# Decoder layer on one core: attention in two halves of 256 tokens with a state between them, and silu as one ScalarE function

## The reference

```python
qkv = silu(x @ qkv_w.T)                      # 32 heads of q, k, v, 128 wide
# linear attention with a decay per head, here written over all pairs of tokens
scores[n, m] = (q[n] . k[m]) * exp(-slope * (n - m))   if n >= m else 0
attn = scores @ v                            # the reference steps over blocks of 64 with a state
attn = attn * rsqrt(mean(attn ** 2) + 1e-5)  # over all heads
x = layernorm(x + (sigmoid(x @ gate_w.T) * norm_w * attn) @ out_w.T)
x = layernorm(x + fake_quant(x) @ fake_quant(ctx_4096))
x = layernorm(x + grouped_ffn(x))            # 16 groups, gelu
```

## Time and profile before

| | us |
|---|---|
| median of three runs (1871.03 to 1873.51) | 1873.34 |
| span of the profiled execution | 1870.5 |
| TensorE busy | 1807.6 (97%) |
| VectorE busy | 1443.7 (77%) |
| ScalarE busy | 940.1 (50%) |
| GpSimd busy | 627.6 (34%) |

### The profile page before, as it was taken

One profiled execution on the slowest core, in us unless ns is written; L12 is line 12 of the kernel. 1 busy time (PEld: TensorE's weight loads), 2 busy tenths in 40 slices (PEclk: granted clock), 3 DMA queues, 4 the chain that ended last, 5 costly groups with the idle time before them and its releaser, 6 DMA issues.

```text
span 1870.5 us, 26340 instructions
## 1 busy us (share of the span) xinstructions
PE 1807.6 (97%) x9325; PEld 872.7 (47%) x9325; DVE 1443.7 (77%) x2029; ACT 940.1 (50%) x1402; POOL 627.6 (34%) x506
## 2 busy tenths in 40 slices
PE   6999999999999999999999999999999999998887
PEld 4444544444444544444444544444444544564433
DVE  7777777778777777778777777778777777669877
ACT  5554544545454545545454545445354544434664
POOL 2352334324342334324342334324342332301423
PEclk9999999999999999999999999999999999999998
DMA  4112223131322223221321213121221213133332
GB/s 174 65 68 91 69 90 90 69 90 46 119 63 90 69 89 91 76 83 46 119 62 57 70 56 90 57 68 46 85 63 57 71 54 91 58 103 122 113 91 90
DMA packets 117792, 149.64 MB, mean 80 GB/s; under 512 B 67232, under 2 KB 83744, under 8 KB 117280
## 3 DMA queue, kind: packets, MB, share of 16 engines
q1 hardware_dynamic: 106208, 135.29, 22.9%
q0 software_dynamic: 2560, 8.39, 1.4%
q10 hardware_dynamic: 8896, 4.28, 0.8%
HBM read 119.63 MB, written 12.58 MB: 71 GB/s over the span
## 4 chain that ended last, share of the span: by engine, by line
PE 77%; DVE 13%; ACT 4%; issue 4%; DMA 1%; POOL 0%; ACTq 0%; DVEq 0%; SPq 0%; POOLq 0%
PE bank L1296 18%; PE bank L1298 17%; PE bank L1297 17%; PE bank L1269 6%; PE bank L1361 4%; PE bank L1363 3%; PE bank L1362 3%; DVE gated_split L1616 3%; PE bank L1338 2%; PE bank L1340 2%; PE bank L1339 2%; DVE acc L1758 2%; PE bank L1425 1%; PE bank L1436 1%; DVE bank L1676 1%
## 5 line engine op out<-in xcount | busy, mean ns | idle before, releaser
L1296 PE MATMUL bank<-x_blocks,w_pair 128*128 128x512 f16 (+1 forms) x1820 | 678.5, 373 | 12.7 <-DVE bank L1664 7.3
L1298 PE MATMUL bank<-x_blocks,w_pair 128*128 128x512 f16 (+1 forms) x1820 | 678.3, 373 | 0.0
L1297 PE MATMUL bank<-x_blocks,w_pair 128*128 128x512 f16 (+1 forms) x1820 | 678.2, 373 | 0.0
L1876 POOL TENSOR_TENSOR sums_pair<-raw_pair 128x512 f32<-128x512 f32 x63 | 87.0, 1380 | 576.5 <-DVE w_pair L1616 414.6
L1296 PEld LDWEIGHTS bank<-x_blocks,w_pair 128*128 128x128 f16 x1820 | 177.9, 98 | 218.2 <-DVE bank L1664 15.0
L1298 PEld LDWEIGHTS bank<-x_blocks,w_pair 128*128 128x128 f16 x1820 | 178.0, 98 | 202.8
L1297 PEld LDWEIGHTS bank<-x_blocks,w_pair 128*128 128x128 f16 x1820 | 178.1, 98 | 191.0
L1758 DVE TENSOR_TENSOR acc<-acc,bank 128x512 f32<-128x512 f32 x320 | 207.8, 680 | 17.5 <-PE bank L1363 17.5
L1537 ACT ACTIVATE scores_split<-bank 128x512 f16<-128x512 f32 (+1 forms) x192 | 100.6, 526 | 180.9 <-DVE bank L1721 160.7
L1616 DVE SCALAR_TENSOR_TENSOR w_pair<-raw_pair,w_pair 128x1024 f16<-128x1024 f32 x126 | 158.0, 1273 | 34.3 <-ACT w_pair L1489 34.1
L1902 POOL TENSOR_TENSOR ssq<-ssq,sig 128x512 f32<-128x512 f32 x64 | 83.4, 1303 | 282.4 <-ACT sig L1543 281.9
(11 more groups left out here) (212 smaller groups left out, 2637.4 us busy)
## 6 DMA issues: line engine op xcount, KB each, us to landing
raw_pair<-w_qk SPq DMA_DIRECT2D x32, 1024.0 KB, 5.0
raw_pair<-w_gate SPq DMA_DIRECT2D x16, 1024.0 KB, 4.9
raw_pair<-w_out SPq DMA_DIRECT2D x16, 1024.0 KB, 4.9
raw_pair<-w_vt SPq DMA_DIRECT2D x15, 1024.0 KB, 4.9
decay_sb<-decay SPq DMA_DIRECT2D x32, 256.0 KB, 5.3
raw_pair<-ctx_in SPq DMA_DIRECT2D x8, 1024.0 KB, 4.8
acc<-x_t SPq DMA_DIRECT2D x4, 1024.0 KB, 11.5
ctx<-raw_pair SPq DMA_DIRECT2D x8, 512.0 KB, 3.4
```

What stands on the lines that cost most here:

```text
L1296: pe.matmul(out, w_hi, x_hi, start=unmet and k == 0, stop=False, skip_group_check=halves or not fresh)
L1297: pe.matmul(out, w_hi, x_lo, start=False, stop=False, skip_group_check=halves or not fresh)
L1298: mm = pe.matmul(out, w_lo, x_hi, start=False, stop=k == QT - 1, skip_group_check=halves or not fresh)
```

## The change

Silu: ScalarE computes the function Silu straight into `sig32` and the two halves are split from there; the VectorE multiply goes, and a bank is free after ScalarE's one read. `sig32` is held until the low half is written.

Attention of pairs 0 to 14: the 512 tokens are taken in two halves of 256. Scores are computed within each half only (256 and 128 columns for each of two key blocks, in two groups). What the second half takes from the first goes through a state of 128 x 128 per unit. The keys of the first half are multiplied by their decay to the half's end on GpSimd (`k_decay`), split (ScalarE, VectorE) and turned by a DMA transpose on SP (`k_turn`); `state` multiplies them with the values on TensorE and its result is split (ScalarE, VectorE); `attend` multiplies the state with the queries of the second half into a second bank, VectorE scales it by the queries' decay (`inter`) and adds it to bank 7 (`joined`), and only then ScalarE squares. The decay rates (128 KB each, two for the keys and two for the queries of a pair) are loaded by SP, and the decay tiles shrink from 256 to 128 KB. Pair 15 keeps the whole attention.

Order: `state(0)` stands behind the first `gate` product, `state(1)` behind `score(2)`; `gated(0)` and `gated(2)` stand behind the next unit's scores; `gate_rest` (two sigmoids) comes before `units(3)` in `q` instead of after stage 1; the products of `v` run 1, 7, 2, 6, 4, 5, 3. `g32` of all four units lies in the key tile. Core of the diff:

```diff
+HALF_GROUPS = ((0, 2), (1, 3))
+H_OFF = {0: 0, 2: HT, 1: 2 * HT, 3: 2 * HT + P}
+N_HALF = 2 * (HT + P)
...
-    "k": {"p1": "e10", "p6": "w1 w2 l", "p3": "c w0"},
+    "k": {"p1": "e10", "p6": "w1 w2 l", "p5": "j0", "p3": "c w0 j1"},
...
-        st = self.add("silu", done=done, place=place, sign=sign, gi=gi, sig_free=self.sig_free[gi], sig=self.tick("sig"),
-                      silu=self.tick("silu"), dst=dst, free=dst_free if isinstance(dst_free, list) else [dst_free],
-                      slot=self.late_slot, hi=self.tick("qkv_hi"))
-        self.sig_free[gi] = st["silu"]
-        return self.tick("qkv_lo")
+        st = self.add("silu", done=done, place=place, sign=sign, gi=gi, sig_free=self.sig_free[gi], silu=self.tick("silu"),
+                      dst=dst, free=dst_free if isinstance(dst_free, list) else [dst_free], slot=self.late_slot,
+                      hi=self.tick("qkv_hi"))
+        lo = self.sig_free[gi] = self.tick("qkv_lo")
+        return gi, st["silu"], lo
...
+        gi, silu, lo = self.silu(done, place, sign, (which, r), [self.qk_free, self.g_split] if which == "k" else
+                                 [self.qk_free, self.q_read])
+        self.release(place, silu)
+        if which == "k" and r % 2 == 0:
+            self.decay_keys(r // 2, gi, lo)
         for b in range(B):
...
+    def decay_keys(self, g, gi, lo):
+
+        self.add("k_decay", g=g, gi=gi, lo=lo, rate=self.rate_ready[g])
+        rate = self.rate_free[g] = self.sig_free[gi] = self.tick("k_rate")
+        self.kd[g] = gi, rate
+
+    def turn_keys(self, g):
+
+        gi, rate = self.kd[g]
+        self.add("k_turn", g=g, gi=gi, rate=rate, free=self.s_free, hi=self.tick("kd_hi"), before=self.q_read)
+        lo = self.sig_free[gi] = self.tick("kd_lo")
+        self.steps[-1]["lo"] = lo
+        self.s_free = self.k_turned[g] = self.tick(f"k_turned{g}", 16)
+
+    def state(self, g):
+
+        i, bank, free = self.main_ring.take()
+        self.add("state", g=g, bank=bank, free=free, turned=self.k_turned[g], v=[t for b in range(B) for t in self.v_done[b][g]],
+                 mm=self.tick("state_mm"), hi=self.tick("st_hi"))
+        self.st_done[g] = self.tick("st_lo")
+        self.main_ring.give(i, self.st_done[g])
+
     def kv_out(self, b, r):
 
         done, place, sign = self.result(r)
-        lo = self.silu(done, place, sign, ("kv", b, r), [self.qk_free, self.g_split, self.late_units_free])
-        self.release(place, lo)
+        _, silu, lo = self.silu(done, place, sign, ("kv", b, r), [self.qk_free, self.g_split, self.late_units_free])
...
+        if not whole:
+            j, st["bank2"], st["free2"] = self.main_ring.take()
+            st["state"], st["rate"] = self.st_done[h % GH], self.rate_ready[h % GH]
+            st["inter_mm"], st["inter"], st["joined"] = self.tick("inter_mm"), self.tick("inter"), self.tick("joined")
+            self.main_ring.give(j, st["inter"])
+            self.rate_free[h % GH] = st["inter"]
+            self.q_read = st["mm"]
         self.s_free = st["mm"]
...
-        if unit == 0:
-            free = [self.g_split, self.g_summed]
-        else:
-            free = [self.scores_mm[1 if unit < 3 else 3]]
...
-                 blocked=blocked, free=free if blocked else [])
+                 blocked=blocked, free=[self.scores_mm[1 if unit < 2 else 3]] if blocked else [])
...
+    def load_rates(self, n, what):
+
+        for g in range(GH):
+            self.add("rate", h=n * GH + g, what=what, free=self.rate_free[g])
+            self.rate_ready[g] = self.tick(f"rate_in{g}", 16)
...
-            "p1": [part(0), part(1)] + [part(2), wo_sum],
-            "p7": [attend(0), gated(0), score(1)],
-            "p6": units(0) + [attend(1), gated(1), score(2)],
+            "p1": [state(0), part(0), part(1)] + [part(2), wo_sum],
+            "p7": [attend(0), score(1), gated(0)],
+            "p6": units(0) + [attend(1), gated(1), score(2), state(1)],
             "p5": [wo(0)],
-            "p4": sums(S3) + [gate(0)] + split_sum(S3) + [wo(1), attend(2), gated(2), score(3)],
+            "p4": sums(S3) + [gate(0)] + split_sum(S3) + [wo(1), attend(2), score(3), gated(2)],
             "p3": [wo(2), gate(1)] + units(2),
         })
...
-            "p1": [attend(3), gated(3)] + units(3),
+            "p1": [attend(3), gated(3)] + gate_rest + units(3),
             "p2": sums(S2) + split_sum(S2) + stages(0) + sums(S1),
-            "p6": stages(1) + split_sum(S1) + sums(S4) + gate_rest + split_sum(S4),
+            "p6": stages(1) + split_sum(S1) + sums(S4) + split_sum(S4),
             "p7": stages(2) + [part(0), part(1)],
             "p3": stages(3) + [part(2)],
         }, (1, 2, 6, 7, 5, 4, 3))
-        plan.load_decay(n * GH)
-        plan.load_decay(n * GH + 1)
+        plan.load_decay(n * GH, last)
+        plan.load_decay(n * GH + 1, last)
         if last:
...
-            "p5": stages(10) + [part(2)],
+            "p5": stages(10) + [part(2)] + [turn(0)],
             "p4": stages(11),
             "p3": [part(0)],
         })
+        plan.load_rates(n, "q")
         product_pair(plan, "v", n, {
-            "p1": stages(12) + [part(1)],
+            "p1": stages(12) + [turn(1), part(1)],
             "p7": stages(13) + [part(2)],
             "p2": stages(14),
             "p6": stages(15) + [lambda: plan.scores(n, UNITS[0])],
-        })
+        }, (1, 7, 2, 6, 4, 5, 3))
...
+            whole, (_, s_hl, off) = st["whole"], c.scores_of(st)
+            if not whole:
+                until(pe, sem, st["free2"])
+                pe.wait_ge(sem["st_lo"], st["state"][1])
+                state = [c.k_t[:, st["h"] % GH, n, b, 0] for n in range(2)]
+                q = c.units["q"][:, st["h"] % GH, :, b, HT:S]
+                three(pe, c.banks[st["bank2"]][:, 0:HT], [(state, (q[:, 0], q[:, 1]))]).then_inc(sem["inter_mm"])
             for j in range(ST):
-                at = slice(S_OFF[j], S_OFF[j] + S - P * j)
-                vh, vl = (c.v_hl[:, j // 2, n, b, j % 2, st["h"] % GH] for n in range(2))
-                sh, sl = c.s_hl[:, 0, at], c.s_hl[:, 1, at]
-                pe.matmul(bank[:, j * P:S], vh, sh, start=j == 0, stop=False)
-                pe.matmul(bank[:, j * P:S], vh, sl, start=False, stop=False)
-                mm = pe.matmul(bank[:, j * P:S], vl, sh, start=False, stop=j == ST - 1)
+                n = width_of(j, whole)
+                at, to = slice(off[j], off[j] + n), slice(j * P, j * P + n)
+                first, last = (j == 0, j == ST - 1) if whole else (j % 2 == 0, j % 2 == 1)
+                vh, vl = (c.v_hl[:, j // 2, n_, b, j % 2, st["h"] % GH] for n_ in range(2))
+                sh, sl = s_hl[:, 0, at], s_hl[:, 1, at]
+                pe.matmul(bank[:, to], vh, sh, start=first, stop=False)
+                pe.matmul(bank[:, to], vh, sl, start=False, stop=False)
+                mm = pe.matmul(bank[:, to], vl, sh, start=False, stop=last)
             mm.then_inc(sem["attend_mm"])
+        elif kind == "state":
+            g, bank = st["g"], c.banks[st["bank"]]
+            until(pe, sem, st["free"])
+            until(pe, sem, st["turned"])
...
+            for token in st["v"]:
+                until(pe, sem, token)
+            for b in range(B):
+                mm = three(pe, bank[:, b * HD:(b + 1) * HD],
+                           [([c.k_t[:, g, n, b, i] for n in range(2)], [c.v_hl[:, 0, n, b, i, g] for n in range(2)])
+                            for i in range(2)])
+            mm.then_inc(sem["state_mm"])
         elif kind == "out":
...
         elif kind == "silu":
-            src = c.placed(st["place"])
             act.wait_ge(sem[st["done"][0]], st["done"][1])
             until(act, sem, st["sig_free"])
-            act.activation(c.sig32[st["gi"]][:, :], src, ACT.Sigmoid, scale=st["sign"] / W_SCALE).then_inc(sem["sig"])
+            act.activation(c.sig32[st["gi"]][:, :], c.placed(st["place"]), ACT.Silu,
+                           scale=st["sign"] / W_SCALE).then_inc(sem["silu"])
+            src = c.sig32[st["gi"]][:, :]
             act.wait_ge(sem["silu"], st["silu"][1])
...
-            dve.wait_ge(sem["sig"], st["sig"][1])
-            dve.scalar_tensor_tensor(out=src, in0=src, scalar=st["sign"] / W_SCALE, in1=c.sig32[st["gi"]][:, :],
-                                     op0=ALU.mult, op1=ALU.mult).then_inc(sem["silu"])
+            src = c.sig32[st["gi"]][:, :]
             dve.wait_ge(sem["qkv_hi"], st["hi"][1])
             for cols, (hi, lo) in c.split_targets(st):
...
+                dve.wait_ge(sem["inter_mm"], st["inter_mm"][1])
+                until(dve, sem, st["sq_free"])
+                until(dve, sem, st["rate"])
+                dve.tensor_tensor(tmp, c.banks[st["bank2"]][:, 0:HT], c.decay_sb[st["h"] % GH][:, HT:S],
+                                  ALU.mult).then_inc(sem["inter"])
+                dve.wait_ge(sem["attend_mm"], st["mm"][1])
+                dve.wait_ge(sem["inter"], st["inter"][1])
```

(5 more changed lines are left out.)

159 lines of the change are left out of this document (112 added, 47 removed).

## The result

| | before | after |
|---|---|---|
| median, us | 1872.3 | 1979.9 (1972.4 to 1983.8) |
| ratio, 95% interval | | 1.057, 1.0546 to 1.0594 |
| mean period of the 14 middle pairs | 105.16 | 112.68 |

A forecast was written before the change was run, and what follows sets the result against it. TensorE, busy for 97% of the span, was taken as the bound. The terms -39.0 + 13.2 + 1.5 + 14.7 - 4.2 + 7.0 = -6.8 us took 1870.5 to 1863.7, given as a 1866.5 us median, range 1836 to 1896.

The forecast's parts named there:

- columns: TensorE's attention matmuls: 6144 fewer columns a pair, saving 2.6 us a pair, 39.0 us over fifteen pairs.
- (A): Product 3 of `v`, now right behind product 5, stalls for `c22`: 0.94 us in 14 pairs, +13.2 us.
- (B): `state(0)` behind the first `gate` product waits for a value transpose: 0.1 us taken, +1.5 us in 15 pairs.
- (D): `attend(3)` needs `gated(2)`: ready at 9.7 us against TensorE's 10.0, so it just fits and adds nothing.
- (E): Output stage 1 in `q` waits for the seed and `S2`'s low half: 1.05 us in 14 pairs, +14.7 us.
- (F): Product 5 of `q` waits for `u3`; a lighter VectorE gives back 0.3 us, 14 times, -4.2 us.
- (G): Output stages 9 to 11 in `k`, delayed by GpSimd's key multiply: net +0.5 us, 14 times, +7.0 us.
- R2: Rival, slower: value transposes land late and `state(0)` holds TensorE 1.5 us; +21 us, 1887.5 us; chance 0.27.
- (C): `attend(1)` needs bank 7, so `gated(0)`: about 5.5 us against TensorE's 6.15; nothing added.
- Tables: ScalarE's function tables: Sigmoid and Silu alternate; upper bound taken, two loads of 1.28 us a pair.
- R3: Rival: a switch of function tables costs twice its row; 36 us more, 1902 us; chance 0.03.
- R1: Rival: the saving stands, since loads and waits in `q` and `k` don't cost; 1851.8 to 1838.8 us; chance 0.17.

The follow-up runs named there:

- the best of the later ones: The halves with silu as before and several orders mended, last v's output stages 14 and 15 one slot later, against the kernel before: 1879.8 us, 1.0030.

## Why the prediction was wrong

It gave 1866.5 us, range 1836 to 1896; it took 1980. No rival held it either. Every wait that it counted came, most of them larger, and none of them alone is the miss. In the 14 middle pairs, by distances of starts (which are up to 0.2 us longer than a wait of the tables), after less before:

| | forecast, us | measured, us |
|---|---|---|
| columns | -36.4 | -32.5 |
| (A) product 3 of `v` | +13.2 | +32.0 |
| (B) `state(0)` | +1.4 | +2.3 |
| (D) `attend(3)` | 0 | +6.5 |
| (E) seed and second product | +14.7 | +46.2 |
| (F) `u3` | -4.2 | -2.4 |
| (G) adds in `k` and `v` | +7.0 | +29.4 |
| lower clock | no term | +23.5 |
| sum | -4.3 | +105.0 |

Point by point:

- **Columns,** -2.6 us a pair: about right, 2.3 in the changed kernel and in the best of the later ones.
- **(A)** product 3 of `v`, 0.94 us a pair. The price of the order is 0.94 exactly, in the runs with the keys on VectorE and with the transpose first. But the changed kernel pays 32.2 us instead of 13.2. The step that failed is the one on SP's queue: "Behind these stand the value transposes and a weight load, both wanted later." It has no term for them. It asked which DMA waits behind which, and not which transfer is under way when a transpose starts. Shown by the run that changes only SP's order. The run with the keys on VectorE shows what made the load late: the key multiply ahead of the weight sums, which the sum priced in (G) alone.
- **(B)** `state(0)` 0.1: right in the changed kernel (0.21 us by start distances, too short for the table of waits). R2's mechanism is real, but in the old order of `v` and with the old silu: 1.58 and 0.79 us.
- **(C)** nothing: right.
- **(D)** nothing, "It just fits": it waited 0.39 us in 12 pairs, 4.6 us. The terms listed don't add up to 9.7: 4.75 and 1.22, 0.8, 1.0, 0.6, 1.1, 0.75 make 10.2, later than TensorE's 10.0. With the right sum the step would have had 0.2 us of wait.
- **(E)** 1.05 a pair: 1.92 + 1.13, and the lower clock behind them. Two rows were missing in the chain: `gate(3)` waits for `gated(3)`, whose tile it overwrites, 0.88 us; and the low halves took 1.20 and 1.75 us beside GpSimd's sums, where I took 0.71 for the first, from a row without GpSimd, though a row with it (1.32) stood beside it. That the loads matter was right (a load of 1.28 us is the upper bound that I took). That a stall lowers the clock for the work behind it had no term at all.
- **(F)** -0.3: in the right direction, 0.44 to 0.20 in the typical pair, but to 0.58 in others; the total went from 7.3 to 6.4.
- **(G)** +0.5 net: the key multiply starts where forecast, and the net cost is 1.8 a pair (29.1 against 3.8 us of such waits before; stage 15 is among them). The mis-sized term is the sums: I took 1.22 and 1.27 for the first two, from a stretch where no split ran beside them; they took 3.47 from the first's start to the second's end, 1.0 more. With that the forecast's wait of 0.93 would have been 1.9, and it was 1.85.
- **Tables:** two loads a pair, 1.28 us each, nothing beside the load. R3 is refuted.

R1's reason, that a lighter VectorE gives waits back, holds for 4 us, shown by silu's split without loads. And VectorE's busy time fell by 75 us, 5 a pair, and not 9: silu's low halves grew from 692 ns, out of a bank, to 832 ns (queries) and 861 ns (keys) in the mean, out of SBUF, and the weights' low halves of 1024 columns from 1273 to 1478 ns, 26 us in 126 of them.

The pattern: each place was found, and each was priced alone, with durations from rows in which it was alone. In the changed kernel the multiply that was added on GpSimd moved sums onto splits, and the load onto a transpose. The two edits that mend one order each gave 37 and 36 us in the medians. The traces show 24 for GpSimd's, nearly all of it waits, and 36 for SP's: 18 of wait, 7 of clock behind it, and 10 of clock in `q`, whose waits didn't change. How often the clock falls behind the same wait differs from run to run, and why stays open. Nor do the parts add up the other way: the changed kernel with its stages later, the scores as cover, the multiply on VectorE and SP's order mended together is 41 us faster, where the multiply alone gave 47.

## What to carry to other kernels

When a change puts an operation ahead of others on an engine, price not only its time but whom its followers will now run beside: a sum on GpSimd beside a split on VectorE, and a load that this split lets go beside a transpose. When TensorE is at 97%, removed columns are worth their time only if no new wait outlasts the TensorE work that covers it; waits of 2 us and more can cost more than themselves. And a new order is to be checked link by link for tiles that are overwritten (`gate(3)` for `gated(3)`, product 7 for `gate(2)`), not only for data that is read.

## What the runs showed of the hardware

- Silu and Sigmoid don't share a table: 16 and 15 loads in the kernel, 1.28 us each, the activation 0.02 us behind the load.
- GpSimd's and VectorE's operations out of SBUF slow each other when they overlap: 1.27 to 2.25 us and 1.25 to 1.78 us. The one that starts second pays: VectorE's split at 740.32 kept its 1.25 us, and the sum that started on GpSimd at 740.56, inside it, took 2.13, ending 1.12 us behind the split. The Trainium skill, SBUF — State Buffer (SBUF: two separate sides), says that a VectorE operation with two SBUF inputs and a GpSimd operation share a port pair, which the one that starts first holds to its end while the other is blocked. The trace agrees: in the three overlaps around stage 10 the later operation ended 1.07 to 1.13 us behind the earlier one, a little under its own 1.25 or 1.27 us.
- A DMA transpose issued 0.6 us behind a 1 MB load landed after 5.8 us in the median, 2.0 us behind it after 4.1, 2.8 us behind it after 3.1, and after 3.1 when it was issued ahead of the load.
- After 1.85 us of work in 4.9, TensorE was granted 0.53 of its clock for 3.2 us. In the changed kernel the lower level came behind 4 of product 3's 5 waits of about 3 us, and behind none of its nine shorter ones (1.4 to 2.3 us). A single wait of 2.2 us (for `gate(2)`) brought it in 8 of 14 pairs, and one of 2.54 us (for stage 2's add) in 8 of 14. Runs of one kernel differ with it: 1921.5 us at a granted clock of 0.992, 1942.5 at 0.978.
